# A graph-transformer kernel on one core: the first group's loads in another order, and its stacking copies shared by two queues

## The reference

```python
# block L0
nx = _ln(x, ln1_g, ln1_b)
q, k, v = (nx @ wq + bq), (nx @ wk + bk), (nx @ wv + bv)        # 8 heads of 32
scores = jnp.einsum('bhqd,bhkd->bhqk', q, k) / np.sqrt(HD) + bias  # bias from adj: 0.1*adj*adj or -inf
out = softmax(scores) @ v
x1 = x + (out @ wo + bo)
x = x1 + gelu(_ln(x1, ln2_g, ln2_b) @ w1 + b1) @ w2 + b2
# graph layers, k = 0, 1
q, kk = x @ Wq[k].T + bq[k], x @ Wk[k].T + bk[k]
attn = softmax over neighbours of q @ kk.T / SCALE
x = layer_norm(x + (attn @ x) @ Wc[k].T, ln_g[k], ln_b[k])
```

## Time and profile before

| | us |
|---|---|
| median of 3 runs | 2107.9 |
| lowest, highest | 2106.68, 2108.05 |
| the profiled execution, its own time | 2108.7 |
| its span in the profile | 2106.5 |
| PE busy in the span | 1875.1 (89%) |
| DVE, ACT, POOL busy | 1699.1, 1563.0, 1020.0 |

### The profile page before, as it was taken

The page is one execution under the profiler, slowest core; times in us unless marked ns, Lnnn a source line. Parts: engine busy times, 40 slices in busy tenths (PEclk is TensorE's granted clock), DMA queues, the critical chain, the costliest instruction groups (busy, mean ns, idle before and its releaser), DMA issues.

```text
span 2106.5 us, 44313 instructions
## 1 busy us (share of the span) xinstructions
PE 1875.1 (89%) x15704; PEld 1350.9 (64%) x15704; DVE 1699.1 (81%) x3398; ACT 1563.0 (74%) x2996; POOL 1020.0 (48%) x1304
## 2 busy tenths in 40 slices
PE   3678899999999999999999999999999999999884
PEld 2545566666666667666667676666667666666662
DVE  3666788888888888888888888898888888888653
ACT  2466677788877777887777778877777788777651
POOL 2012235555544555555455555544554555445575
PEclk9688899999999999999999999999999999999997
DMA  6223344333344443333444433344544333444311
GB/s 147 52 53 91 91 101 101 95 83 85 91 101 111 111 101 87 85 86 96 101 111 103 104 83 82 86 108 101 111 101 99 85 80 91 110 102 86 66 36 40
DMA packets 441610, 192.46 MB, mean 91 GB/s; under 512 B 347760, under 2 KB 416368, under 8 KB 441392
## 3 DMA queue, kind: packets, MB, share of 16 engines
q1 hardware_dynamic: 440848, 188.82, 38.2%
q0 software_dynamic: 544, 0.80, 0.3%
HBM read 38.55 MB, written 16.78 MB: 26 GB/s over the span
## 4 chain that ended last, share of the span: by engine, by line
PE 61%; ACT 14%; DVE 10%; POOL 9%; issue 4%; SPq 1%; DMA 1%; DVEq 0%; POOLq 0%; ACTq 0%
PE ps L327 16%; PE ps L329 16%; PE ps L328 16%; PE ps L1277 6%; POOL area L534 4%; PE ps L1342 3%; DVE st L729 2%; ACT L666 2%; ACT cs L687 2%; DVE area L742 2%; POOL hid_l L334 2%; DVE area L881 2%; ACT L687 2%; POOL rs L529 2%; POOL ve L527 2%
## 5 line engine op out<-in xcount | busy, mean ns | idle before, releaser
L645 ACT ACTIVATE area<-area,nmax 128x128 f32<-128x128 f32 x1024 | 312.6, 390 | 19.5 <-DVE nmax L856 18.8
L527 POOL TENSOR_TENSOR ve<-mv,eps_cols 128x4 f32<-128x4 f32 x128 | 62.2, 486 | 482.0 <-DVE mv L734 481.8
L334 POOL TENSOR_TENSOR hid_l<-area,hid_h 128x512 f16<-128x512 f32 x128 | 156.2, 1220 | 284.8 <-ACT hid_h L669 284.8
L327 PE MATMUL ps<-w_h,hid_h 128*128 128x256 f16 x1024 | 279.4, 273 | 12.1 <-POOL hid_l L334 12.1
L329 PE MATMUL ps<-w_h,hid_l 128*128 128x256 f16 x1024 | 279.2, 273 | 0.0
L328 PE MATMUL ps<-w_l,hid_h 128*128 128x256 f16 x1024 | 279.1, 273 | 0.0
L666 ACT ACTIVATE area<-ps,b_col 128x512 f32<-128x512 f32 x256 | 176.0, 687 | 45.0 <-PE ps L329 38.2
L327 PE MATMUL ps<-rot_h,w_h 128*128 128x512 f16 x512 | 198.9, 388 | 8.6 <-ACT area L666 5.4
L329 PE MATMUL ps<-rot_h,w_l 128*128 128x512 f16 x512 | 198.5, 388 | 0.0
L328 PE MATMUL ps<-rot_l,w_h 128*128 128x512 f16 x512 | 198.5, 388 | 0.0
L534 POOL TENSOR_TENSOR area<-area,cwb_row 128x256 f32<-128x256 f32 x128 | 90.8, 739 | 197.7 <-ACT area L695 197.7
(11 more groups left out here) (200 smaller groups left out, 5903.6 us busy)
## 6 DMA issues: line engine op xcount, KB each, us to landing
qkS<-qk SPq DMA_DIRECT2D x384, 128.0 KB, 2.3
xin<-in_x SPq DMA_DIRECT2D x32, 512.0 KB, 4.5
adj_in<-in_adj SPq DMA_DIRECT2D x64, 256.0 KB, 2.9
out<-x SPq DMA_DIRECT2D x30, 512.0 KB, 2.8
area<-in_L_gnn_w SPq DMA_DIRECT2D x1, 1024.0 KB, 8.5
area<-in_L_gnn_w SPq DMA_DIRECT2D x2, 512.0 KB, 12.4
rot_h<-sA_h SPq DMA_TRANSPOSE x64, 2.8
rot_l<-sA_l SPq DMA_TRANSPOSE x64, 2.7
```

What stands on the lines that cost most here:

```text
L327: pe.matmul(dst, lh, rh, start=start, stop=False, **kw)
L334: eng.tensor_tensor(hid_l[:, c % RING, :], hidden[:, c % 2, :], hid_h[:, c % RING, :], ALU.subtract).then_inc(done, 1)
L645: last = act.activation(sc[:, b % 2, h], sc[:, b % 2, h], ACT.Exp, bias=nmax[:, b, h:h + 1])
```

## The change

SP's list of the first group is put in another order. wo leaves `weights`; `more_weights` is cut into three: `weights_of_layers` (wo and the six loads of the graph layers) stands behind the two transposes of the first group, `weights_up` (w1) behind its stacking copies, and `weights_down` (w2) behind the load of x of the second group. wo gets a semaphore of its own, `ld_wo`. Of the first group's 12 stacking copies SP issues six (j = 0, 1) and ACT the other six (j = 2, 3), the latter at the head of `Q.v1`. ACT's high halves of w1 move from `Q.v1` to `A.exp1`, DVE's remainders of w1 from `Q.mA` to `A.S2`, and the counts BO_MADE and B1_MADE follow. The loop and the end are not touched.

```diff
         PREP_DVE = 18 + len(halves)
         BQK_MADE = 3 + HALVES_QKV + 4
         BV_MADE = BQK_MADE + 1
-        BO_MADE = BV_MADE + HALVES_W1 - HALVES_QKV + 4
-        B1_MADE = BO_MADE + 1
+        BO_MADE = BV_MADE + HALVES_QKVO - HALVES_QKV + 4
+        B1_MADE = BO_MADE + HALVES_W1 - HALVES_QKVO + 1
...
-                for n, w in enumerate((wq, wk, wv, wo)):
+                for n, w in enumerate((wq, wk, wv)):
                     sp.dma_start(raw_qkvo[:, n], w.rearrange("(c p) n -> p c n", p=P)).then_inc(ld_raw[0], 16)
 
-            def more_weights():
-                sp.dma_start(raw_w1, w1.rearrange("(c p) n -> p c n", p=P)).then_inc(ld_raw[1], 16)
+            def weights_of_layers():
+                sp.dma_start(raw_qkvo[:, 3], wo.rearrange("(c p) n -> p c n", p=P)).then_inc(ld_wo, 16)
                 for l in range(L):
...
+            def weights_up():
+                sp.dma_start(raw_w1, w1.rearrange("(c p) n -> p c n", p=P)).then_inc(ld_raw[1], 16)
+
+            def weights_down():
                 for n in range(2):
...
                         turn(g, xT_h, xT_l, sN_h, sN_l, a_xT, d_xT, m_xT)
+                        if g == (0, 0):
+                            weights_of_layers()
...
                         if g == (0, 0):
                             weights()
+                        elif g == (0, 1):
+                            weights_down()
...
-                            for j in range(4):
+                            for j in range(2 if g == (0, 0) else 4):
                                 sp.dma_start(qkS[32 * slot:32 * slot + 32, :, j],
                                              qk16[32 * j:32 * j + 32, parts]).then_inc(stk, 16)
+                        if g == (0, 0):
+                            weights_up()
...
                         sp.dma_start(adj_in[:, :, :], rows(adj_dram, g)).then_inc(ld_adjA, 16)
-                        if g == (0, 0):
-                            more_weights()
...
                 elif step == "Q.v1":
+
+                    for i in range(4):
+                        act.wait_ge(d_qk[i], 1)
+                    for slot, parts in enumerate((slice(0, 3, 2), slice(0, 4, 3), slice(1, 3, 1))):
+                        for j in range(2, 4):
+                            act.dma_start(qkS[32 * slot:32 * slot + 32, :, j],
+                                          qk16[32 * j:32 * j + 32, parts]).then_inc(stk, 16)
+                    act.wait_ge(ld_wo, 16)
                     highs(HALVES_QKV, HALVES_QKVO)
+                    act.wait_ge(const_ok, 6)
+                elif step == "A.exp1":
                     act.wait_ge(ld_raw[1], 16)
                     highs(HALVES_QKVO, HALVES_W1)
-                    act.wait_ge(const_ok, 6)
-                elif step == "A.exp1":
                     act.wait_ge(prep_pe, 2)
...
                 elif step == "Q.mA":
-                    lows(HALVES_QKV, HALVES_W1)
+                    lows(HALVES_QKV, HALVES_QKVO)
...
                 elif step == "A.S2":
+                    lows(HALVES_QKVO, HALVES_W1)
                     dve.wait_ge(prep_pe, 4)
...
                     last.then_inc(prep_pe, 1)
                     pe.wait_ge(prep_dve, BV_MADE)
+                    pe.wait_ge(ld_wo, 16)
```

More of the change, by code:

```diff
@@ L218, in graph_blocks @@
         ld_raw = [sem(f"ld_raw{n}") for n in range(4)]
-        ld_ln, ld_bias, ld_vec = sem("ld_ln"), sem("ld_bias"), sem("ld_vec")
+        ld_wo, ld_ln, ld_bias, ld_vec = sem("ld_wo"), sem("ld_ln"), sem("ld_bias"), sem("ld_vec")
         const_ok = sem("const_ok")
@@ L598, in prepare @@
                     act.wait_ge(prep_dve, 3)
-                    act.wait_ge(ld_raw[0], 16 * 4)
+                    act.wait_ge(ld_raw[0], 16 * 3)
                     highs(0, HALVES_QKV)
@@ L955, in prepare @@
                     pe.wait_ge(ld_ln, 16 * 4)
-                    pe.wait_ge(ld_raw[0], 16 * 4)
+                    pe.wait_ge(ld_raw[0], 16 * 3)
                     for t in range(6):
```

## The result

| | before | changed |
|---|---|---|
| median | 2108.05 | 2104.51 us |
| lowest, highest of 17 runs each | 2103.93, 2113.32 | 2100.55, 2107.12 |
| ratio, 95% interval | | 0.9981 (0.9974 to 0.9988) |
| the profiled execution, its span | 2108.7, 2106.5 | 2106.19, 2103.9 |

The change gains 4.0 us by the ratio (2.5 to 5.5), which is about the bound of what counts as a difference here.

The account below looks back on a forecast made before the run. The loop keeps TensorE busy 1685 of 1810 us; its start waits for queued transfers, then stacking copies. 10.0 + 0.9 - 0.6 - 1.2 = 9.1 us off 2107.9 gave 2098.8 us, range 2094.5 to 2105.0.

Parts of the forecast that it names:

- The transposes ahead of the late weights: First group's start: transposes issued before the late weights, xT_l landing at 20.3 instead of 30.3; gain 10.0 us.
- The sum: All parts of the change added: 10.0 + 0.9 - 0.6 - 1.2 = 9.1 us gained, median 2098.8 us; chance 0.50.
- The bounds 4.7 and 12.2: Transposes at the start: least gain if xT_l still takes 10.3 us to land, most if 2.8 us.
- rival C: At the start, POOL's broadcasts hold the transposes as the weights did: gain 3.8 us, 2104.1 us; chance 0.20.
- Half of the stacks on ACT: First group's stacking copies issued from two queues, limited by DMA engines already 0.88 busy: gain 0.9, bounds 0 and 3.1.
- rival B: Stacking copies limited by their issue, two queues doubling their pace: 6.6 us to first scores, 2096.0 us; chance 0.15.
- rival E: At the stacking copies, ACT's issues are held by full queues: slower, 2111.5 us; chance 0.03.
- x behind w1: Second group's x, loaded behind w1, lands at 57.8 where DVE asks at 57.2: loss 0.6, bounds 0 and 1.8.
- w1's halves: First block's preparation: w1's high halves and remainders made later on ACT and DVE delay b_col: loss 1.2, bounds 0 and 3.4.
- The carry, one for one: From start through loop: whatever starts the loop earlier moves all of it and its end by the same amount.
- The prediction's own test: From b_col to the span's end: a distance differing by more than 1 us would make the prediction wrong.

Follow-up runs that it names:

- the one line in the kernel before: Kernel before the change, with only POOL's small columns and six row broadcasts made to wait for the first group's two transposes: 2099.48 us, ratio 0.9965.
- the crossed one: Changed kernel, SP issuing stacking copies into slots 0 and 1, ACT slot 2 with sources in order 2, 3, 0, 1: 2108.33 us, single execution.
- the rows early: Changed kernel with POOL's six row loads issued at the very start, right behind the three bias columns: 2096.84 us, ratio 0.9946 to the kernel before.

## Why the prediction was wrong, point by point

**The transposes ahead of the late weights: +10.0 forecast, +5.8 measured.** This is the step that failed. The sum put xT_l's landing at 20.3, with POOL's 0.79 MB counted as 2.0 us at the 402 GB/s of the bulk loads. It landed at 24.4 (15.22 + 9.2). Bytes over the rate of other loads was the wrong price: the rows moved at 50 to 90 GB/s from 17 to 20, and the transposes stood still meanwhile. The 4.2 us between 10.0 and 5.8 are nearly all of what the sum was off by at `b_col` (9.1 against 4.85). What in the loads makes their packets slow stays open. The bounds 4.7 and 12.2 held. The evidence that was read for it, that the pair landed 3.1 us after the last of w2, showed only that both ended together: most of what it took for w2's backlog was POOL's, as the one line in the kernel before showed (8.1 us for TensorE's start, 7.1 for w2 itself). The row that had it, 12.4 us for the last of the rows, was given to rival C, with a chance of 0.20 and 2104.1 us; 2104.5 came. C had the mechanism; that its time came so close is in part luck: its parts were off both ways (4.7 at the transposes for 5.8, 0.9 for 0.2 at the stacks, −0.6 for 0 at x), and the change is measured to 1.5 us either way only.

**Half of the stacks on ACT: +0.9 forecast, +0.2 measured** (9.69 to 9.47). The mechanism was right, a full set of DMA engines. The share rose from 0.88 to 1.07, but the GB/s only from 203 to 229, and the last copies landed 5.2 to 5.5 us after their issue instead of 2.35. The size was off: 0.9 was the whole missing share, as if each packet still cost the same, and 0.2 came. The 6.6 us of rival B didn't come. Issues by ACT weren't held (4.06 us for six), so rival E fell.

By the Trainium skill, page "SBUF — State Buffer", section "Door 1: The DMA port swizzle (why [64,N] ≈ [32,N])", an estimate for copies that write 32 partitions is 218 GB/s; the 229 here, 219 of them the copies', agree. By its table partitions 0 to 63 and 64 to 127 reach different ports. That crossed copies go at up to twice the rate was this document's theory P and is not on that table; the 237 GB/s measured don't show it.

**x behind w1: −0.6 forecast, 0 measured** in the changed kernel: SP, with six issues fewer, sent it early enough, if barely (issued at 43.89, landed 7.9 us later at 51.8, read at 51.93). The price was there: 1.1 us without the split, 1.73 with the crossed one.

**w1's halves: −1.2 forecast, −1.3 measured** on the path from the scores to `b_col`, and 0.3 of it had been paid before the scores in the other place, so −1.0 net.

**The sum to `b_col`** is 5.8 + 0.15 (q and k) + 0.2 − 1.3 = 4.85, and 4.0 came (2.5 to 5.5).

**The carry, one for one: right.** 11.3 us at `b_col` gave 12.9 in the median (8.6 to 15.6 by the interval), 8.0 gave 8.5, 11.9 gave 11.5 (the rows early). The traces show it step by step. How much earlier than before stands the same step of DVE, a group's adjacency work, and at the end its last normalisation:

| in the kernel before at | 98.20 | 160.15 | 343.46 | 1129.30 | 1190.79 | 1916.02 | 2096.10 |
|---|---|---|---|---|---|---|---|
| changed | 4.78 | 4.09 | 3.00 | 2.77 | 3.82 | 3.38 | 2.60 |
| changed, POOL's loads late | 11.37 | 11.27 | 11.22 | 11.16 | 12.21 | 12.26 | 11.23 |
| before, POOL's loads late | 8.04 | 8.00 | 7.97 | 7.92 | 8.11 | 7.70 | 7.96 |

In the last two rows the loop carries the whole shift, but for 1.05 us between 1129 and 1191 in the upper one, where the clock fell in the kernel before (below). The prediction's own test, that the distance from `b_col` to the end must stay within 1 us, failed in the profiled pair, where 4.85 at `b_col` became 2.6 at the end; no part of the change is in between. At three places where the shift changes, the granted clock differs between the two traces; the others were not followed. The kernel before, at these three (TensorE's clock is the third number from the end):

```profile
95.00:105.00 10.00, 7.50 (x36) 5.40 (x37) 3.08 (x5) 0.84 (x1) 0.00 (x0) 0.55 0.53 120
180.00:190.00 10.00, 9.20 (x42) 5.19 (x41) 5.67 (x9) 7.08 (x11) 2.24 (x3) 0.70 0.30 73
1147.00:1153.00 6.00, 5.76 (x26) 3.86 (x27) 5.71 (x21) 5.94 (x14) 5.27 (x8) 0.72 0.65 152
```

and the changed one, where the same work stands:

```profile
90.20:100.20 10.00, 7.51 (x31) 5.24 (x32) 2.95 (x4) 0.86 (x1) 0.00 (x0) 0.50 0.53 120
175.90:185.90 10.00, 9.20 (x38) 4.98 (x37) 5.36 (x8) 6.74 (x10) 2.25 (x3) 0.63 0.29 71
1144.20:1150.20 6.00, 5.18 (x31) 3.36 (x32) 5.71 (x21) 5.94 (x14) 5.26 (x8) 1.00 0.60 145
```

At 0.50 it is the lower level, 1.2 GHz, at 1.00 the upper. At the first two places the changed kernel had the lower clock for longer and lost some 0.7 us at each; at the third the clock fell in the kernel before alone, and the changed one won 1.05. Where it falls and rises differs from execution to execution: over all traces what lies between `b_col` and the end moved from 2.8 us lost to 3.5 won against the kernel before. So the test of 1 us was finer than one pair of executions can answer, and its failing doesn't speak against the carry.

## What to carry to other kernels

When a transfer lands late, look in single microseconds at which queue's packets fill the DMA engines meanwhile; what stands ahead of it in its own queue is only the first suspect. A price of bytes over the best rate seen holds for the loads that reached that rate: rows broadcast by POOL moved at less than a quarter of it just while the transposes waited, and quicker elsewhere. And a load that nobody needs soon (DVE first reads these rows 27 us or more after their issue) is moved behind, or well ahead of, the one that all wait for: one line in POOL's list brought 8.0 us at `b_col`, the change as a whole 4.85.

## What the runs showed of the hardware

DMA transposes nearly stopped beside POOL's row loads: 4 to 10 of their packets in a microsecond, against 615. Packets of a broadcast of one 1 KB row to 128 partitions cost 0.5 to 0.6 us there, those of loads of 128 different rows 0.16; in other microseconds the broadcasts' packets took 0.10 and 0.17 us as well.

DVE is slower beside POOL's issuing of DMAs: the normalisation of the first group took 1.94 us beside POOL's column issues and 1.38 without them, in every trace of either kind. By the Trainium skill, page "SBUF — State Buffer", section "SBUF: two separate sides", VectorE and GpSimd share one pair of ports as an exclusive lock; the two durations are in line with that, though no row shows the ports. Its warning there, that a VectorE operation starves the transfers that POOL issues, isn't the cause of the slow packets from 18 to 20 in the changed kernel, since DVE did nothing from 17.9 on.

Two queues copying between on-chip partitions gained 0.2 us against one (9.69 to 9.47 from the first copy to the scores), and 1.0 where their reads and writes kept to different halves of the partitions (8.67 and 8.69).
